# Gated cross-attention with mixture-of-experts on one core: new step lists that put scores in pairs, and both ends of the program rewritten

## What is computed

```python
x = x + tanh(g_xattn[0]) * attn(layernorm(x), ctx)      # qh, kh, vh = projections; softmax(qh kh^T / 8) vh; @ Wo + bo
x = x + tanh(g_ffn[0]) * moe(layernorm(x))

# moe(x):
probs = softmax(x @ gate_w.T)                           # [tokens, 8]
routing_weights, selected = top_k(probs, 2)
comb = sum over the 2 of one_hot(selected) * routing_weights
out = sum over e of (x @ expert_w[e].T + expert_b[e]) * comb[:, e]
```

## Time and profile before

| | |
|---|---|
| runs | 1048.35 us median of 3 (1048.29 to 1058.73) |
| the profiled execution | 1048.92 us, span 1047.1 us |
| PE busy | 1002.5 us, 96% of the span |
| DVE busy | 846.3 us, 81% |
| ACT busy | 792.6 us, 76% |
| POOL busy | 627.3 us, 60% |
| DMA queue | 83.7% of 16 engines' time |

### The profile page before, as it was taken

The page is one execution under the profiler, slowest core; times in us unless marked ns, Lnnn a source line. Parts: engine busy times, 40 slices in busy tenths (PEclk is TensorE's granted clock), DMA queues, the critical chain, the costliest instruction groups (busy, mean ns, idle before and its releaser), DMA issues.

```text
span 1047.1 us, 29286 instructions
## 1 busy us (share of the span) xinstructions
PE 1002.5 (96%) x10710; PEld 773.6 (74%) x10710; DVE 846.3 (81%) x1525; ACT 792.6 (76%) x1404; POOL 627.3 (60%) x372
## 2 busy tenths in 40 slices
PE   6789999999999999999899999999999999999998
PEld 5467777787777877778677787777777787777786
DVE  6767788978888878978599788897888887897738
ACT  4899998857986599857798579875798759975600
POOL 4798767536774467654576456754677446754500
PEclk9899999999999999999899999999999999999999
DMA  4999999868996699965999759966799759996630
GB/s 137 169 206 187 169 183 181 129 112 159 176 167 121 101 178 179 160 129 95 167 171 152 129 103 193 179 123 122 131 197 166 129 101 164 177 150 125 112 61 21
DMA packets 554309, 152.13 MB, mean 145 GB/s; under 512 B 541976, under 2 KB 551600, under 8 KB 554160
## 3 DMA queue, kind: packets, MB, share of 16 engines
q1 hardware_dynamic: 554160, 150.18, 83.7%
HBM read 11.70 MB, written 4.19 MB: 15 GB/s over the span
## 4 chain that ended last, share of the span: by engine, by line
PE 71%; DVE 10%; issue 6%; ACT 5%; DMA 4%; POOL 3%; SPq 1%; DVEq 0%; ACTq 0%; POOLq 0%
PE MB L1028 34%; PE ST L1139 16%; PE PV L1155 14%; PE MB L1040 3%; DVE nmax L838 3%; POOL p_s L524 2%; DMA pt_s<-p_s 2%; ACT pf L676 2%; DVE acc L801 2%; ACT p_s L686 1%; DMA pt_s<-wv 1%; PE ST L1164 1%; PE MB L1105 1%; DVE m L971 1%; DVE ot_s L827 1%
## 5 line engine op out<-in xcount | busy, mean ns | idle before, releaser
L524 POOL TENSOR_TENSOR p_s<-pf,p_s 128x1024 f16<-128x1024 f32 x256 | 549.8, 2148 | 319.7 <-ACT p_s L686 313.1
L838 DVE TENSOR_REDUCE nmax<-ST 128x2 f32<-128x1024 f32 x256 | 311.2, 1218 | 52.8 <-PE ST L1139 50.3
L676 ACT ACTIVATE pf<-ST,shifts 128x512 f32<-128x512 f32 x512 | 325.5, 694 | 4.8 <-POOL p_s L524 1.4
L686 ACT ACTIVATE p_s<-pf 128x1024 f16<-128x1024 f32 x256 | 273.0, 1067 | 5.9 <-DMA pt_s<-p_s 2.6
L1155 PEld LDWEIGHTS PV<-v_s,pt_s 128*128 128x128 f16 x6144 | 201.7, 97 | 87.1 <-issue 75.2
L1155 PE MATMUL PV<-v_s,pt_s 128*128 128x65 f16 x6144 | 230.5, 194 | 11.5 <-DVE o_n L854 8.4
L1028 PE MATMUL MB<-ex_s,x2t_s 128*128 128x512 f32 x708 | 190.6, 405 | 1.0 <-DVE QL L818 1.0
L801 DVE SCALAR_TENSOR_TENSOR acc<-MB,m,acc 128x256 f32<-128x256 f32 x236 | 113.7, 482 | 44.9 <-PE MB L1028 34.2
L1028 PEld LDWEIGHTS MB<-ex_s,x2t_s 128*128 128x128 f32 x708 | 125.8, 189 | 29.3 <-issue 2.9
L1139 PE MATMUL ST<-KH,QH 64*128 64x512 f32 x512 | 126.1, 488 | 17.9 <-ACT pf L676 10.9
L667 ACT ACTIVATE shifts<-nmax 128x2 f32<-128x2 f32 x256 | 53.6, 212 | 91.8 <-DVE nmax L838 91.0
(11 more groups left out here) (130 smaller groups left out, 1086.1 us busy)
## 6 DMA issues: line engine op xcount, KB each, us to landing
pt_s<-p_s SPq DMA_TRANSPOSE x512, 3.4
xin<-x SPq DMA_DIRECT2D x7, 512.0 KB, 4.4
out<-acc SPq DMA_DIRECT2D x7, 512.0 KB, 3.5
kvin<-kv_t SPq DMA_DIRECT2D x8, 256.0 KB, 3.5
acc<-expert_t SPq DMA_DIRECT2D x6, 256.0 KB, 3.8
pf<-wq SPq DMA_DIRECT2D x1, 768.0 KB, 8.2
xin<-x SPq DMA_DIRECT2D x2, 256.0 KB, 2.9
pt_s<-wk SPq DMA_DIRECT2D x1, 512.0 KB, 6.7
```

What stands on the lines that cost most here:

```text
L524: pool.tensor_tensor(p_s[:, slot, 1, :, :], pf[:, u % 2, :, :], p_s[:, slot, 0, :, :], ALU.subtract).then_inc(p_lo, 1)
L676: last = act.activation(pf[:, u % 2, i, :], ST[u % 2][:, i, :], ACT.Exp, bias=shifts[:, u % 2, i:i + 1], scale=SCALE)
L686: act.activation(p_s[:, it.ring(p, u, P_SLOTS), 0, :, :], pf[:, u % 2, :, :], ACT.Copy).then_inc(p_hi, 1)
L838: dve.tensor_reduce(nmax[:, t % 2, :], ST[t % 2][:, :, :], AX.X, ALU.max, negate=True)\
```

## The change

1. All four tables are new. `PE_ORDER` now often has the scores of two units directly behind one another ("pairs"), and `NORMALISE_BACK` is 4.
2. The router's weights lie as `[high | low]` side by side, so that two matmuls give high and low products as 16 rows, and two more add the high weights by the low tokens; the `logits` matmuls sum the two halves with a matrix `fold`. The first two wait only for the high parts of the tokens.
3. The start: in batch 0 the second unit's scores go ahead of the second pair's projections; the low part of `wq`'s rest is made by POOL alone; `wv`'s high part comes later on ACT; two small constants on DVE move behind the second unit.
4. The end: the probabilities of the last two units are turned by PE from `pf` and split into parts by ACT and DVE out of `ST`, without copy, `low` and DMAs; units 28 and 29 use a free bank for their values; the last `wo` is done in two halves, one for each head pair; of dummy matmuls 26 stand there where there were 53 (14 for 24 in the wait for the second norm).

```diff
 PE_ORDER = (
-    "scores", "scores values v2,0 v0,0 v1,0", "scores values v3,0", "scores values ot6 values", "scores k2 k3 values",
+    "scores", "scores values v3,0 values v0,0 v2,0", "scores values", "scores values v1,0 k2 values", "scores",
...
+    "scores values v1,1 router ot1 values", "scores values logits ot0 q5 v3,1 values", "scores",
+    "scores values k5 wo0,1 k6 values", "scores", "scores values wo0,0 q6 values", "scores",
...
 ACT_ORDER = (
...
+    "shift copy hi exp copy", "shift hi exp hi", "shift copy exp hi copy", "shift exp", "shift copy exp copy hi",
...
-MAXIMUM_BACK, NORMALISE_BACK = 0, 3
+MAXIMUM_BACK, NORMALISE_BACK = 0, 4
...
-BUSY_VALUES = 3
+ON_PE = UNITS - 2
-BUSY_EPI = {("ot", PAIRS - 1): 3, ("wo", ROUNDS - 1, 0): 6, NEXT_X2T: 24, ("router",): 5, ("logits",): 3}
+BUSY_EPI = {NEXT_X2T: 14, ("router",): 5, ("logits",): 3}
...
+DEFERRED = [NEXT_JOBS[PRO_JOBS:PRO_JOBS + 1], NEXT_JOBS[PRO_JOBS + 1:]]
...
+def in_first(rows, n, late):
+    parts = rows[n].split()
+    if n > 1:
+        return parts
+    if n == 0:
+        return [part for part in parts if part != late]
+    return [part for part in parts if part != late] + [part for part in rows[0].split() + parts if part == late]
...
+        def values_bank(it, m):
+            if it.kind == LAST and m // 2 == ON_PE // 2 - 1:
+                return SHARED[Iteration(EPI, BATCHES, BATCHES % LOOPED).bank(LATE_JOBS[2])]
+            return PV
...
             pool.wait_ge(w_hi, 4)
-            pool.tensor_tensor(wq_s[:, 1, 1, rest], stage_q[:, 1, rest], wq_s[:, 0, 1, rest].bitcast(F32),
-                               ALU.subtract).then_inc(wq_rest_lo, 1)
...
-                if name == ("k", 0):
-                    dve.wait_ge(w_hi, 4)
-                    dve.tensor_tensor(wq_s[:, 1, 0, rest], stage_q[:, 0, rest], wq_s[:, 0, 0, rest].bitcast(F32),
-                                      ALU.subtract).then_inc(wq_lo, 1)
...
+                if kind == FIRST and n == 2:
+                    constants()
...
+            for m in range(ON_PE, UNITS):
+                act.wait_ge(tail_turned, m - ON_PE + 1)
+                act.wait_ge(pv_ready, unit_count(BATCHES - 1, *divmod(m, TT)))
+                act.activation(turned_by_pe(last_batch, m, 0), ST[m % 2][:, :, :], ACT.Copy).then_inc(tail_hi, 1)
...
+            def low_of_last(m):
+                dve.wait_ge(tail_hi, m - ON_PE + 1)
+                dve.tensor_tensor(turned_by_pe(last_batch, m, 1), ST[m % 2][:, :, :], turned_by_pe(last_batch, m, 0),
+                                  ALU.subtract).then_inc(tail_lo, 1)
...
                 elif kind == "router":
-                    last = parts(m[0:EXPERTS, :], [((gt_s[:, 0, c, :], gt_s[:, 1, c, :]),
-                                                    (x2t_s[:, 0, c, :], x2t_s[:, 1, c, :])) for c in range(LC)])
+                    for c in range(LC):
+                        pe.matmul(m[0:2 * EXPERTS, :], gt_s[:, c, :, :].rearrange("p a e -> p (a e)"),
+                                  x2t_s[:, 0, c, :], start=(c == 0), stop=False)
+                    pe.wait_ge(job_free, it.last_done(JOBS, ("x2t", 0), ("x2t", 1)) + BANKS)
+                    for c in range(LC):
+                        last = pe.matmul(m[0:EXPERTS, :], gt_s[:, c, 0, :], x2t_s[:, 1, c, :], start=False,
+                                         stop=(c == LC - 1))
...
+            turn_last(ON_PE)
+            turn_last(ON_PE + 1)
+            for m in range(UNITS - VALUES_BACK, ON_PE):
+                values(last_batch, m)
+            produce(epi, LATE_JOBS[0])
+            for m in range(ON_PE, UNITS):
+                values(last_batch, m)
+            outputs_last(epi, 0)
+            produce(epi, LATE_JOBS[1])
+            keep_busy(4)
+            outputs_last(epi, 1)
```

More of the change, by code:

```diff
@@ L81 @@
[L81 to L85, removed]
@@ L87 @@
+    "shift exp hi copy", "shift exp copy", "shift exp", "shift hi copy exp hi copy", "shift hi exp",
+    "shift copy exp context copy", "shift exp norm1 copy", "shift hi exp hi hi", "shift copy exp",
+    "shift hi copy exp hi copy", "shift exp hi", "shift copy exp hi copy", "shift hi exp", "shift copy exp copy",
 )
 DVE_ORDER = (
-    "maximum", "maximum take", "maximum normalise take take", "maximum take normalise take", "maximum take",
-    "maximum normalise", "maximum take take take normalise", "maximum take take", "maximum take",
@@ L544, in row @@
                     if part == "low":
-                        low(it, *divmod(n, TT))
+                        if it.kind != LAST or n < ON_PE:
+                            low(it, *divmod(n, TT))
                     elif part == "residual":
@@ L629, in row @@
                 b, kind = it.b, it.kind
-                parts = ACT_ORDER[n].split()
-                if kind == FIRST and n == 0:
-                    parts.sort(key=lambda part: part == "hi")
-                for part in parts:
+                for part in in_first(ACT_ORDER, n, "hi") if kind == FIRST else ACT_ORDER[n].split():
                     at = count.get(part, 0)
@@ L908, in row @@
                 b, kind = it.b, it.kind
-                for part in DVE_ORDER[n].split():
+                if kind == FIRST and n == 2:
+                    constants()
+                for part in in_first(DVE_ORDER, n, "take") if kind == FIRST else DVE_ORDER[n].split():
                     at = count.get(part, 0)
@@ L917, in row @@
                             maximum(b, *divmod(at, TT))
-                        if kind == FIRST and at == 0:
-                            for name in JOBS[PRO][PRO_JOBS:]:
+                        if kind == FIRST and at < 2:
+                            for name in DEFERRED[at]:
                                 take_first(name)
@@ L1070, in produce @@
                 elif kind in ("router", "logits"):
-                    before = {"router": [("x2t", 0), ("x2t", 1)], "logits": [("router",)]}[kind]
-                    pe.wait_ge(job_free, it.last_done(JOBS, *before) + BANKS)
+                    if kind == "router":
+                        pe.wait_ge(job_hi, it.last_done(HI, ("x2t", 0), ("x2t", 1)))
+                    else:
+                        pe.wait_ge(job_free, it.done(JOBS, ("router",)) + BANKS)
+                    if kind == "logits":
+                        pe.wait_ge(const_pool, CONST_POOL)
                 elif kind == "gates":
@@ L1129, in produce, with outputs_last @@
                 last.then_inc(job_ready, 1)
+            def outputs_last(it, k):
+                pe.wait_ge(job_free, it.done(JOBS, LATE_JOBS[k]) + BANKS)
+                pe.wait_ge(o_ready, head_count(BATCHES - 1, HEADS - 2) + 1)
+                for name in LATE_JOBS[2:]:
+                    if k == 0:
+                        pe.wait_ge(job_free, it.free_wait(name))
+                    for i in range(2):
+                        q, dst = tile(2 * name[2] + i), SHARED[it.bank(name)][:, DIM * i:DIM * (i + 1)]
+                        w = (ROUNDS - 1) * GROUP + k
+                        for n, (a, c) in enumerate(((0, 0), (0, 1), (1, 0))):
+                            last = pe.matmul(dst, ot_s[:, a, k, q], wo_s[:, c, w, :],
+                                             start=(k == 0 and n == 0 and i == 0),
+                                             stop=(k == GROUP - 1 and n == 2 and i == 1))
+                    if k == GROUP - 1:
+                        last.then_inc(job_ready, 1)
             def scores(it, p, t):
@@ L1190, in row @@
                         scores(it, p, u)
-                        if kind == FIRST and n == 0:
-                            for name in JOBS[PRO][PRO_JOBS:]:
+                        if kind == FIRST and n < 2:
+                            for name in DEFERRED[n]:
                                 produce(pro, name)
```

139 lines of the change are left out of this document (87 added, 52 removed), and 10 rows, old and new, of the table PE_ORDER.

## The result

The changed kernel is slower by about 1%: 1063.78 us (median of 8 runs, 1063.31 to 1065.43) against 1051.58 us for the kernel before in the same comparison (8 runs, 1048.29 to 1058.73), a ratio of 1.0108 with a 95% interval of 1.008 to 1.0136. The forecast was 1034.

What follows compares the result with a forecast made beforehand. PE was taken to bound batches 1 to 7, busy 121.47 of 122.29 us. From 1048.92, batches 7.7, start 1.4 and end 5.3 came off: 1034.5 for the profiled execution, 1034 us at the median; range 1026 to 1045.

Steps and rivals of the forecast that it cites:

- The batches: Batches of the loop: PE's list 1.6 us shorter, less 0.5 of waits: 1.1 us each, 7.7 for seven.
- Net 0.5 us of waits more, bounds 0 and 1.6.: PE in each batch: 1.1 us of new waits, less about half of 1.1 us behind normalisings.
- The router's job: PE in each batch: four matmuls instead of six, 1.39 us down to 0.93, 0.46 less.
- The pairs' own waits: PE in each batch: second scores wait 0.8 us for an exponential, values of unit 14 wait 0.3; 1.1 us.
- The bound of 13 us for seven batches: Upper bound on the gain of seven batches, forecast at 7.7 us; lower bound 0.
- the hold for `bo_t`: Batch 0: DVE's `bo_t` took 2.12 us, ending just behind POOL's subtraction; at its new place a few tenths to 2.3.
- The start: Batch 0: ACT reaches the third exponential earlier, at about 30.6 instead of 32.01; 1.4 us won, bounds 0 and 2.8.
- The end: From the last scores on: 5.3 us won, bounds 3.5 and 6.5.
- the router's matmuls there: At the end, two router matmuls instead of six stand behind the tokens' low parts: 0.9 us won.
- The clock falls at the end: Rival: a gap before the second norm's transposes halves PE's clock; one fall costs 2.5 us, 1036.5 in all; chance 0.10.
- The pairs wait for ACT: Rival: second scores of ten pairs wait 0.8 us each, 8 us a batch, 1086 us; chance 0.11 for above 1044.

Runs made afterwards that it cites:

- after_free: The changed kernel with the routing's small products and the kmax product replaced by reductions, routing weights constant: 1032.80 us, ratio 0.9835 to the kernel before.
- before_free: The kernel before with the routing's small products and the kmax product replaced by reductions, routing weights constant: 1044.28 us, ratio 0.994.
- after_kmax: The changed kernel with only the product of kmax and wv_max moved from DVE into a PE matmul: 1064.93 us, ratio 1.0134.
- after_later: The changed kernel with the routing steps moved down about one row in DVE's table: 1067.36 us, ratio 1.0135.
- after_early: The changed kernel with the routing steps split and put ahead of the maximum in DVE's rows 14, 16, 17 and 18: 1049.39 us, ratio 0.996.
- new_end: The kernel before with only the new end and the router in four matmuls, start and lists as before: 1042.12 us, ratio 0.9924.
- after_early_lean: after_early with the kmax product moved into a PE matmul and the last two routing products made one instruction: 1046.65 us, ratio 0.9968.

## Why the prediction was wrong

**The batches.** This is the step that failed: "Net 0.5 us of waits more, bounds 0 and 1.6." From it came a batch 1.1 us shorter and 7.7 us in all; measured, batches 1 to 6 are 2.9 us longer each, and in batch 2 PE idles 2.8 us more (2.2 to 5.0). Of the step's own terms none was far off. The router's job now (PE, start and duration):

```profile
422.51 0.63 PE L1156 MATMUL MB<-x2t_s,gt_s 128*16 128x512 f32 x2
422.98 0.62 PE L1160 MATMUL MB<-x2t_s,gt_s 128*8 128x512 f32 x2
423.44 0.60 PE L1091 MATMUL MB<-ident,o_n 128*128 128x128 f32 x4
```

0.93 us from start to the next job's start, as forecast. PE's busy time without the hold falls by 1.6 us (121.91 to 120.30). The pairs' own waits, put at 1.1 us a batch, make 7.5 us in some six batches of after_free. With most of the hold gone a batch gets 1.25 us shorter by the profiles; the forecast said 1.1.

The term that was missing is the one that decides. By batches 1 to 6, the hold costs 0.9 us a batch before (124.4 against 123.5) and 5.0 after (127.3 against 122.25). The net, +4.1, turns -1.25 into +2.9. (By the medians the 5.0 can be 0.7 smaller. The clock has a part of some 0.3 us in the 0.9 and in the 5.0, an estimate from 6.8 us at half clock in the six batches against 3.4 without the hold; in the net it cancels.) My bound of 1.6 for new waits came from pairs, ACT and the DMA; from DVE it had none, since DVE had nearly 20 us a batch to spare. It still has 18 of 126.5. What counted was not its share but a delay of 2 or 4 us in its one queue, right ahead of a take. The reading of the kernel before had the same blind spot: it took the 122.29 us of the earlier trace rows for a batch, with PE next to never idle, while batches 1, 2 and 5 took 2 us more; in before_free batches 2 and 5 take 122.4. The bound of 13 us for seven batches does not follow from its terms either: 1.8 and 0.46 without any wait make 2.3 a batch and 16 in all.

I had the mechanism in hand and applied it at one place only. The prediction took the hold for `bo_t` in the start (2.12 us beside POOL's subtraction) and did not ask which of some twenty small operations per batch would meet a low part when both lists move. The Trainium skill, "SBUF — State Buffer", "SBUF: two separate sides", gives the rule: a vector instruction in a two-port mode, or one with two SBUF inputs while GpSimd reads SBUF, takes turns with GpSimd at one pair of ports, and whoever started first keeps it for the whole instruction. The traces agree as far as they go: products of two SBUF operands, the scaling `m<-m,tg` and the conversion `comb_w<-m` are held, with ends that match POOL's within 0.06 us; reductions and operations on PSUM are not. Which mode an instruction ran in, no trace here shows. As an estimate from POOL's 75.3 busy us in 126.5, a randomly placed small product meets a low part six times in ten.

**Where the delay falls** is the second half of the cause, and the runs show it apart from the first. The 12.8 us of the product behind kmax cost nothing measurable (after_kmax); 18 us lie between two places of the same steps (after_later and after_early), against the order of their held time. That what stands next in DVE's list, and how soon PE needs it, decides the cost is read from PE's waits in these traces; no run moves a take alone.

**The start** was put at 1.4 us, bounds 0 and 2.8. Batch 0 is 2.6 us longer in the changed kernel's profile. The third exponential comes at 31.38, not 30.6; 32.01 before. `bo_t` took 0.35 us at its new place, free of POOL. So the third exponential came 0.6 us earlier, not 1.4, and batch 0 still did not get shorter. The experiments give both signs, so this term was neither shown nor refuted; it is small beside the other.

**The end** was right in its sum, 5.3 us forecast and 5.7 measured, but two of its terms were off and cancel. PE at the last scores, the last values and the second norm's transposes:

```profile
1008.85 0.40 PE L1215 MATMUL ST<-KL,QH 64*128 64x512 f32 x2
...
1017.99 1.63 PE L1237 MATMUL PV<-v_s,pt_s 128*128 128x65 f16 x48
...
1029.45 1.65 PE L1091 MATMUL MB<-ident,xn 128*128 128x128 f32 x8 [1.59 <-DVE xn L776]
```

From the last scores to the last values' end 10.4 us (forecast 10.8, before 14.3), to the transposes 20.2 (21.4, before 25.8). By the timeline they started at 25.6 before (1014.22), so the way to them won 5.4 us where 4.4 were forecast. Behind their start it took 32.9 us before and 32.6 after: 0.3 us in place of the 0.9 that were put down for the router's matmuls there.

**The rivals.** *The clock falls at the end*: not in the changed kernel's profile, with a gap of 1.59 us ahead of the transposes and a granted clock of 1.00 from 1004 to 1060 us. But behind the same gap (1.57 us) it did fall in three other profiles with the new end, new_end, after_early and after_early_lean. In new_end:

```profile
1006.25 1.83 PE L1079 MATMUL MB<-ident,xn 128*128 128x128 f32 x8 [1.57 <-DVE xn L764]
1007.60:1011.02 3.42, 3.42 (x16) 2.75 (x15) 1.31 (x2) 1.09 (x2) 0.00 (x0) 0.50 0.02 5
```

One such fall costs 1.5 us, not 2.5: the end takes 54.3 us in after_early and 52.8 in the changed kernel. So this rival is real and small, and that the changed kernel was spared is luck. The Trainium skill, "TensorE: Matmul & The Clock Gate", "Part 4: PE-mode transpose", says that transposes do not count as busy the way matmuls do. These rows neither show nor refute it: the 16 new transposes stand among matmuls, and the clock was at 1.00 behind them. *The pairs wait for ACT* was the right sign with the wrong mechanism: these waits sum to 4.8 us in some six batches of the changed kernel and 2.4 in after_free, where that rival had 8 us in each batch. It had a chance of 0.11 for anything above 1044, and nothing covered a slower kernel through DVE.

## What to carry to other kernels

When a change moves lists on two engines that can hold each other up, list the small operations of the one against the long instructions of the other, not only the chain of the bound engine: an operation of 0.19 us can take the other's 2.15. Ask of each what stands right behind it and how soon that is needed; here neither DVE's busy time nor the total held ranked the kernels. And if such steps must stay in a statically ordered queue, first try other rows for them: here that moved the time by 18 us, more than the change itself. The fastest of these kernels that still compute the routing is the new end and the router in four steps on the old lists, with two operations less on DVE: 1037.07 us.

## What the runs showed of the hardware

- A VectorE product of 128x32 numbers in SBUF takes 0.19 us alone and up to 2.12 us beside a GpSimd subtraction of 2.15 us. A product of 128x1 is held as well: 1.78 us beside a subtraction of 3.47. So the size does not protect it.
- A held product and a held scaling behind one another (1.91 and 2.18 us) each waited for one of two low parts that followed one another without a gap. The first got through between the two low parts, the second did not; so it was in seven of eight batches (means 1694 and 1945 ns over the eight).
- A `tensor_reduce` with SBUF source of the same size was never long: mean 177 to 187 ns in all groups of 128x32 in after_free, in the same rows of the list.
- One SBUF input does not protect either: the conversion `comb_w<-m` of 128x64 numbers took 0.20 us alone and about 1.5 us beside a low part, in seven of eight batches of after_free; the scaling `m<-m,tg` took 0.24 us alone and 2.2 us beside one, in seven of eight batches of the changed kernel.
